# Moving an attention output projection from a pair's first period into its second

## The reference, cut to what matters

```python
# once per batch; the input x is layer-normalised first
q = (x @ Wq)  # 16 heads x 64
k, v = context @ Wk, context @ Wv
attn = softmax(q k^T * 64 ** -0.5)          # 256 x 4096 per head
out = attn @ v                              # 256 x 1024
x = x + out @ Wo + bo
```

## Time and profile before

| | us |
|---|---|
| three runs, median (lowest, highest) | 2188.32 (2187.38, 2191.1) |
| the profiled execution's own time | 2186.71 |
| its span in the profile | 2184.9 |
| TensorE matmul busy | 2035.5 (93%) |
| VectorE busy | 1471.7 (67%) |
| GpSimd busy | 1422.2 (65%) |
| ScalarE busy | 1304.1 (60%) |

### The profile page before, as it was taken

How to read it: one execution, slowest core, us unless ns; L and a number is a source line. 1 busy time by engine, 2 the same in 40 slices (tenths; PEclk the granted TensorE clock), 3 DMA queues, 4 the chain that set the end, 5 groups by cost and what they waited for, 6 DMA issues and landing times. The chain is left out here.

```text
span 2184.9 us, 47341 instructions
## 1 busy us (share of the span) xinstructions
PE 2035.5 (93%) x19706; PEld 1492.2 (68%) x19706; DVE 1471.7 (67%) x1834; ACT 1304.1 (60%) x1574; POOL 1422.2 (65%) x683
## 2 busy tenths in 40 slices
PE   4799999989999999999999999999999976779998
PEld 3577777767777777677777776777777743335466
DVE  5666666776666667666666676666666615987757
ACT  2476767766767677767676767676767652010233
POOL 0277777777777777677777777777777763633327
PEclk8899999999999999999999999999999988889999
DMA  8010101120101011201011121001010003003212
GB/s 239 15 35 7 35 14 42 33 57 14 28 14 28 14 43 33 56 14 28 14 28 27 29 56 33 26 16 28 14 28 4 4 4 149 0 1 104 89 52 75
DMA packets 47763, 83.51 MB, mean 38 GB/s; under 512 B 7329, under 2 KB 31521, under 8 KB 46785
## 3 DMA queue, kind: packets, MB, share of 16 engines
q1 hardware_dynamic: 47552, 80.47, 13.2%
HBM read 73.70 MB, written 5.31 MB: 36 GB/s over the span
## 5 line engine op out<-in xcount | busy, mean ns | idle before, releaser
L765 POOL TENSOR_TENSOR acc<-acc,PR 128x1024 f32<-128x1024 f32 x480 | 1155.2, 2407 | 344.2 <-ACT PR L546 306.8
L621 DVE TENSOR_REDUCE amx<-ps 128x2 f32<-128x1024 f32 x512 | 626.8, 1224 | 386.0 <-PE ps L319 386.0
L546 ACT ACTIVATE PR<-ps 128x1024 f32<-128x1024 f32 x512 | 518.5, 1019 | 234.1 <-PE ps L327 234.1
L506 ACT ACTIVATE ps<-NM 128x1024 f32<-128x1024 f32 x416 | 427.1, 1028 | 189.4 <-DVE V L606 145.0
L335 PE MATMUL ps<-PR,V 128*64 128x256 f32 x4096 | 503.7, 388 | 0.1
L335 PEld LDWEIGHTS ps<-PR,V 128*64 128x64 f32 x4096 | 273.2, 137 | 162.8 <-issue 32.6
L327 PE MATMUL ps<-qh,KH 64*128 64x256 f32 x2048 | 328.0, 309 | 32.3 <-ACT ps L506 29.3
L301 PE MATMUL ps<-wv,C 64*128 64x256 f32 x4608 | 314.5, 280 | 0.0
L301 PEld LDWEIGHTS ps<-wv,C 64*128 64x128 f32 x4608 | 305.0, 187 | 8.4
L290 PE MATMUL ps<-C,wk 64*128 64x512 f32 x2304 | 309.7, 396 | 1.0 <-DVE x L655 1.0
L327 PE MATMUL ps<-ql,KH 64*128 64x256 f32 x2048 | 299.8, 279 | 0.0
(11 more groups left out here) (191 smaller groups left out, 1774.1 us busy)
## 6 DMA issues: line engine op xcount, KB each, us to landing
wk<-wk_split SPq DMA_DIRECT2D x62, 192.0 KB, 3.2
wv<-wv_split SPq DMA_DIRECT2D x30, 384.0 KB, 5.2
bc<-wm_rows SPq DMA_DIRECT2D x32, 256.0 KB, 4.2
craw<-in_ctx SPq DMA_DIRECT2D x30, 256.0 KB, 3.9
we<-in_we SPq DMA_DIRECT2D x10, 768.0 KB, 4.4
wo<-in_wo SPq DMA_DIRECT2D x68, 64.0 KB, 2.2
wq<-in_wq SPq DMA_DIRECT2D x32, 128.0 KB, 3.0
craw<-in_ctx SPq DMA_DIRECT2D x30, 128.0 KB, 4.0
```

The lines of the kernel that those rows point to most:

```text
L506: act.activation(ps[:, first_bank:first_bank + 2, :].rearrange("p h (k n) -> p h k n", k=2), row.unsqueeze(2).to_broadcast([P, 2, 2, ROWS] ...
L546: act.activation(PR[:, pr_slot(t, hf), :, :, :].rearrange("p h k n -> p (h k n)"), ps[:, bank:bank + 2, :].rearrange("p h n -> p (h n)"), ...
L621: dve.tensor_reduce(amx[:, :, t, c], psG, AX.X, ALU.max).then_inc(g_max, 1)
L765: pool.tensor_tensor(flat(acc[:, :, :, :]), flat(acc[:, :, :, :]), flat(PR[:, pr_slot(t, hf), :, :, :]), ALU.add).then_inc(acc_done, 1)
```

## The change

TensorE issues `project_out` in the second period (s = 1), behind round 0 of the next pair's maximum and ahead of the second half of the scores. It was issued at s = 0 behind the projection of the queries. VectorE's `add_rows` moves with it, to behind the maximum of round 0. The wait of the job for x_added moves from s = 0 to s = 1, and at s = 0 the job waits for the drained bank in its place.

```diff
--- before.py
+++ after.py
@@ -420,14 +420,15 @@
                             if last and pi == 1:
                                 pe.wait_ge(xn_in, (b + 2) * 16)
                             project_q(nslot)
+                        scores_of(t, 0)
+                    if rounds[0] is not None:
+                        next_guess(rounds[0])
+                    if s == 1:
                         pe.wait_ge(ot_ready, p + 1)
                         pe.wait_ge(wo_in[pi], (it + 1) * 32)
                         if has_job(t - 1, final):
                             wait_drained(pe, it, t - 1, 1)
                         project_out(pi)
-                        scores_of(t, 0)
-                    if rounds[0] is not None:
-                        next_guess(rounds[0])
                     scores_of(t, 1)
                     if rounds[1] is not None:
                         next_guess(rounds[1])
@@ -443,8 +444,10 @@
                             pe.wait_ge(cready, b * 4 + 4 + job[2] + 1)
                         if s == 0:
                             pe.wait_ge(q_ready, p + 2)
-                            pe.wait_ge(x_added, p + 2)
+                            wait_drained(pe, it, t - 1, 1)
                         else:
+                            if s == 1:
+                                pe.wait_ge(x_added, p + 2)
                             pe.wait_ge(p_ready, 2 * T + 1)
                             wait_drained(pe, it, t - 1, 1)
                         project(job, low_bank(t), psB,
@@ -698,7 +701,6 @@
                             split_q(1 - pi, p + 1)
                         dve.wait_ge(seeded, 2 * T + 2)
                         dve.tensor_copy(NM[:, :, :].rearrange("p h n -> p (h n)"), psN).then_inc(nm_sb, 1)
-                        add_rows((p + NC - 2) // NC, p)
                         dve.wait_ge(p_ready, 2 * T + 2)
                         dve.wait_ge(nm_sb, p + 1)
                         dve.tensor_copy(ps[:, score_bank(t, 1) + 1, :].rearrange("p (k n) -> p k n", k=2),
@@ -706,11 +708,15 @@
                     if s == 3:
                         copy_l(p)
                     if more:
-                        for n in ROUNDS[s][0:3]:
+                        for i, n in enumerate(ROUNDS[s][0:3]):
                             if n is not None:
                                 chunk_max(p + 1, n)
+                            if s == 1 and i == 0:
+                                add_rows((p + NC - 2) // NC, p)
                         if s == NC - 1:
                             negate_max(p + 1)
+                    elif s == 1:
+                        add_rows((p + NC - 2) // NC, p)
                     if s == NC - 1:
                         invert_l(p)
                     if has_job(t, final):
```

## The result

The changed kernel takes 2203.68 us (median of 4 runs, 2201.14 to 2205.38) against 2189.09 of the kernel before on the same occasion (2187.38 to 2191.1): ratio 1.0065, 95% interval 1.0048 to 1.0083, so 14.6 us slower. 2212 us had been forecast, in a range of 2198 to 2219. The profiled execution has a span of 2202.0 us against 2184.9, 17.1 longer.

What follows compares the result with a forecast made beforehand. TensorE's instructions in a row, plus short waits at the head, were taken as the bound. Even pairs 15.5, ordinary odd 4.0, three behind a refresh 3.6, last 0.9 summed to +24.0 us: 2212, range 2198 to 2219.

Steps and rivals of the forecast that it cites:

- Even pair: ... gain 0.49 us: Head (s = 0) of pairs with pi = 0: the job starts at +3.43 instead of +3.92 us.
- Odd pair: ... gain 1.13 us: Head (s = 0) of pairs with pi = 1: the job starts at +3.44 instead of +4.57 us.
- a pair costs what TensorE's instructions take one behind the other: Attention part: TensorE, busy 491.24 of 500 us, sets a pair's length, plus short waits at its head.
- a way to be wrong: Head: seeds for the second period's scores, or q_ready, hold TensorE; then odd pairs gain less.
- Cost 2.51 - 1.05 = 1.46 us: Period 2 (s = 1): job later behind round 0, 1.21 us from TensorE's own work and 0.25 from waiting for x_added.
- Pairs behind a refresh: Pairs 7, 15, 23, following a context refresh: head gains 0.48 us, s = 1 costs 1.2 each; 3.6 us in all.
- The last pair: No rounds there; ScalarE's exponential waits for scores behind project_out: +1.07 less 0.19 at its head, +0.9 us.
- 1 (no wait for x_added): Period 2: add_rows done sooner or chunk_max starts sooner, so s = 1 costs 1.21; +16 us, 2204; chance 0.17.
- 2: Period 2: later second-half exponential, sum and buffer release cost some 0.3 us per pair more; +33 us, 2222; chance 0.11.
- 3: Period 2: add_rows collides with GpSimd's summing, +40 us on top, 2252; chance 0.02.
- 4: Not slower: project_out fills lost TensorE time at s = 1; deciding cost 0.72 us; 6 us less, 2182; chance 0.03.
- 5: The head's lead removes other TensorE waits, 20 us back: about +4, no measurable change; chance 0.05.

Runs made afterwards that it cites:

- The parities taken apart: Two runs, the changed order in even pairs alone and in odd pairs alone: 2201.85 and 2197.12 us, against 2188.01 of the kernel before.
- The cut jobs: Changed kernel and kernel before, each without a third of the first period's job's matmuls: 2203.01 and 2187.17 us, against 2187.23 of the uncut kernel before.
- The short project_out: Changed kernel with project_out's matmuls in period 2 computing 32 of 256 columns: 2202.87 us against 2187.77 of the kernel before, ratio 1.0072.
- project_out ahead of round 0: Changed kernel with project_out ahead of round 0 in period 2 and add_rows ahead of its maximum: 2198.43 us against 2188.01 of the kernel before.
- a filler of six: Changed kernel with six extra matmuls of project_out's size behind the queries' projection in pairs 7, 15, 23: 2200.95 us against 2187.77 of the kernel before.

## Why the prediction held, and where its sum was off

- **Slower, as the move costs more in period 2 than it gives back at the head.** Right in direction and in this mechanism: at the head project_out filled time in which TensorE would have waited for seeds, and in period 2 next to nothing hides it. The parities taken apart show both terms.
- **"Even pair: ... gain 0.49 us", "Odd pair: ... gain 1.13 us".** This term was mis-sized: 0.66 and 1.35 to round 0. The forecast took the job's start as the measure, with the instructions behind it in a row on TensorE. The job did gain what was forecast (0.54 and 1.18), but the head is bound by another chain: first scores, two exponentials, VectorE's seed, second scores, 3.83 to 3.85 us in either kernel (2.36 to 6.19 and 1.68 to 5.53 in an even pair, 3.03 to 6.87 and 1.69 to 5.52 in an odd one). The gain is therefore that of the first scores, 2.36 - 1.68 = 0.68 and 3.03 - 1.69 = 1.34. The cut jobs show it, and with it that the step "a pair costs what TensorE's instructions take one behind the other" was wrong at the head. That seeds might hold TensorE there was named as a way to be wrong, with the opposite sign: they held it before as well.
- **"Cost 2.51 - 1.05 = 1.46 us".** To the job it was 2.42 - 1.05 = 1.37; the release by add_rows took 0.73 us (1071.81 to 1072.54), not the 0.82 taken from pair 7. 0.10 more came back behind the job, as period 3's scores had waited for ScalarE's seed in the kernel before; in the kernel after that chain (scores 1.16 later, exponential, seed) and the job's end meet within 0.1 us: 1.27 in all. The short project_out and project_out ahead of round 0 move one of the two chains each. That x_added is waited for, and that it is VectorE's order and not TensorE's work which sets the job, was right.
- **Sum.** 15 even pairs at 0.97 and 12 odd ones at 0.33 would be 18.5; those terms' two errors, 0.17 to 0.22 and 0.19, make some 0.4 us on each of 27 pairs, 10 to 11 us. Measured are 6.2 for 12 even and 12 odd ones, and 2.1 for the three even ones with a refresh.
- **Pairs behind a refresh**, 3.6 forecast, 6.8 in the profile: some 4.1 at full clock, by the run with a filler of six, and 2.7 with the clock. The forecast held them at full clock because in the profile before they were. It was luck that this error, of the other sign, covered part of the one above: without it the whole would have been some 3 us less, near 2200.5, close to the lower end of the range. Pair 0 was forecast at +0.97 and was 0.5 shorter: it has half clock at its head (0.50 from 84.7 to 88.8 us before), where project_out took 1.85 us, so the head gave back 1.75 us up to round 0, and period 2, at full clock, cost 1.27. That part is read from rows, no run isolates it. The last pair cost 1.5 for the 0.9 forecast; the granted clock of its first 16.3 us was 0.78 in the profile after and 0.90 before, and whether that is the cause was not tested.
- **Rivals.** 1 (no wait for x_added) was wrong in mechanism, though its 2204 is the time measured. 2 and 3 did not occur: add_rows took 0.68 us beside a busy GpSimd, and ordinary pairs cost less, not more. 4 is out, as period 2's cost of 1.27 is above the point that decides. 5 named the right kind of thing, a head whose lead removes waits, but looked for them in TensorE's visible idle time, which did not shrink (8.76 us in 500 before, 10.44 after); what the head gave beyond the forecast came from the chain through the seeds, whose wait the visible idle time does not hold.

## What to carry to other kernels

Busy time next to 98% did not mean that TensorE was the bound at every point: its last matmuls cover short waits. So compare the start of an instruction with the end of what it could wait for, and a constant distance (0.11 to 0.12 us here) is the sign of a dependence. Follow the chain across engines from the moved instruction to the next point where all meet, and price the move there, not at the next instruction on the same engine; a cut that leaves the time unchanged tells which chain it is. An instruction that seems to delay others may stand in time that would be lost anyway, and by filling it also keep the matmul clock up: see what the engine does without it. And before a difference between two profiles is put down to an edit, see in other profiles of like kernels whether that part repeats.

## What the hardware showed that was not expected

A third of the first period's job, 12 or 6 matmuls and 0.7 us of TensorE in each pair, left out: 2187.17 against 2187.23 us. The granted clock fell to one half behind 2.0 to 2.7 us without a matmul in 11 of 18 heads and behind 3.3 to 4.0 us in all 15, but also behind 1.22 us in five of twelve executions of pair 30, while behind 0.8 to 1.1 us it stayed full in all three heads seen. In the heads of the kernel after the pairs with a fall took 57.93, 58.78 and 57.75 us, against 57.38, 57.25 and 57.15 with six filler matmuls.
